# Second attention of a six-stage network: sums over the values in blocks of four steps instead of two, with eight buffers of probabilities instead of six

## The reference, cut to what matters

```
q, k = rope(x @ w_q.T), rope(x @ w_k.T);  v = x @ w_v.T
p = softmax(q @ k.T / sqrt(8))            # 512 x 512 for each head
out = x + concat_heads(p @ v) @ w_o.T
```

## Time and profile before

| | |
|---|---|
| time, median of 3 runs | 1658.82 us (1653.32 to 1661.22) |
| profiled execution, its own time | 1665.16 us |
| its span | 1663.4 us |
| TensorE busy | 1481.2 us (89%) |
| VectorE busy | 1036.2 us (62%) |
| ScalarE busy | 913.6 us (55%) |
| second attention, first scores to last sums | 1217.33 to 1434.41 us |

### The profile page before, as it was taken

How to read it: one execution, slowest core, us unless ns; L and a number is a source line. 1 busy time by engine, 2 the same in 40 slices (tenths; PEclk the granted TensorE clock), 3 DMA queues, 4 the chain that set the end, 5 groups by cost and what they waited for, 6 DMA issues and landing times. The chain is left out here.

```text
span 1663.4 us, 23904 instructions
## 1 busy us (share of the span) xinstructions
PE 1481.2 (89%) x7768; PEld 679.3 (41%) x7768; DVE 1036.2 (62%) x2527; ACT 913.6 (55%) x1706; POOL 495.0 (30%) x429
## 2 busy tenths in 40 slices
PE   7899999899988989879999986899889999878995
PEld 3444444344433333324434442268422222336663
DVE  6677775111117999966667765934368988186653
ACT  6866666524668999641046673012218888533443
POOL 5202111000137998820012221035101221006881
PEclk9999999999999999999999998999879999799998
DMA  6112210300000000010021119111222220242333
GB/s 161 49 30 59 68 30 2 98 0 1 0 5 3 4 5 5 0 48 1 1 51 27 27 35 398 32 17 22 92 81 68 73 68 21 86 150 33 43 42 86
DMA packets 64079, 84.21 MB, mean 51 GB/s; under 512 B 12442, under 2 KB 54992, under 8 KB 61942
## 3 DMA queue, kind: packets, MB, share of 16 engines
q1 hardware_dynamic: 55814, 75.85, 14.9%
q0 software_dynamic: 8144, 6.85, 3.3%
HBM read 54.09 MB, written 24.08 MB: 47 GB/s over the span
## 5 line engine op out<-in xcount | busy, mean ns | idle before, releaser
L697 ACT ACTIVATE a_probs_sb<-a_t_ps 128x512 f32<-128x512 f32 x512 | 286.1, 597 | 102.3 <-PE a_t_ps L545 56.4
L798 DVE CUSTOM_DVE_ANT_0 a_biased<-a_s_ps,a_bias 128x512 f32<-128x512 f32 x256 | 165.2, 686 | 65.9 <-issue 65.7
L541 PE MATMUL a_t_ps<-a_stack 126*128 126x512 bf16 (+1 forms) x512 | 164.1, 394 | 18.0 <-ACT a_probs_sb L697 6.6
L805 DVE TENSOR_REDUCE a_least_sb<-a_s_ps 128x2 f32<-128x1024 f32 x128 | 153.1, 1221 | 24.6 <-PE a_s_ps L522 23.7
L1597 POOL TENSOR_TENSOR s_dbu<-s_du,s_bs 128x1024 f32<-128x1024 f32 x64 | 152.2, 2389 | 26.1 <-DVE s_h L1678 20.1
L522 PE MATMUL a_s_ps<-a_stack 96*128 96x512 bf16 (+1 forms) x512 | 148.8, 393 | 12.2 <-DMA a_stack<-a_stacks 8.2
L1678 DVE TENSOR_TENSOR_SCAN s_h<-s_ps,s_dbu 128x512 f32<-128x512 f32 x128 | 149.0, 1205 | 6.4 <-ACT s_ps L1460 6.4
L559 PE MATMUL a_o_ps<-a_probs_sb,a_vpad 128*16 128x512 f32 x1024 | 132.0, 611 | 0.1
L1209 PE MATMUL s_ps<-s_hc,ident 128*128 128x512 f32 x256 | 120.5, 592 | 1.2 <-DVE s_hc L1685 1.2
L2093 ACT ACTIVATE q_probs_sb<-q_s_ps,q_most_sb 128x512 f32<-128x512 f32 x128 | 86.5, 683 | 48.1 <-DVE q_most_sb L2171 47.2
L1460 ACT ACTIVATE s_ps<-s_delta,s_decay 128x511 f32<-128x511 f32 x128 | 85.8, 686 | 27.5 <-DVE s_h L1678 27.2
(11 more groups left out here) (525 smaller groups left out, 2780.8 us busy)
## 6 DMA issues: line engine op xcount, KB each, us to landing
x_wu<-in_x_wu SPq DMA_DIRECT2D x2, 4096.0 KB, 17.4
a_stacks<-a_p SPq DMA_DIRECT2D x16, 384.0 KB, 3.3
a_stack<-a_stacks SPq DMA_DIRECT2D x32, 192.0 KB, 3.9
a_stack<-a_stacks SPq DMA_DIRECT2D x64, 96.0 KB, 2.3
a_stacks<-a_p SPq DMA_DIRECT2D x16, 256.0 KB, 2.4
q_q<-q_q SPq DMA_DIRECT2D x32, 128.0 KB, 2.3
x_wd<-in_x_wd SPq DMA_DIRECT2D x2, 2048.0 KB, 33.3
c_w<-in_c_w SPq DMA_DIRECT2D x2, 2048.0 KB, 12.7
```

The costliest lines, as they stand in the source:

```text
L541: last = nc.tensor.matmul(out, operand(1, k, pair, e, TURNED_ROWS)[:, t * P:(t + 1) * P], operand(0, k, pair, e, TURNED_ROWS), start=True, ...
L697: nc.scalar.activation(probs[:, y % PROB_RING, e, :], bank("turned", y, e), ACT.Exp, scale=-1.0).then_inc(probs_ready, 1)
L798: nc.vector.tensor_tensor_reduce(out=biased[:, e, :], in0=s_ps[:, 2 * (x % 2) + e, :], in1=bias[:, h, at:at + N], scale=1.0, scalar=3.0e38 ...
L805: nc.vector.tensor_reduce(least[:, k % 2, both], s_ps[:, 2 * (x % 2):2 * (x % 2) + 2, :], axis=AX.X, op=ALU.min).then_inc(least_ready, 1)
```

## The change

The sums of four steps are made together, at x divisible by 4; the other even steps have none. The ring of probabilities grows from six to eight buffers, since the oldest of them are now read up to two steps later. Nothing is computed otherwise, and no instruction is added or removed.

```diff
-    LAG, SUM_LAG, PROB_RING, SUM_STEPS = (13, 4, 8, 4) if alibi else (14, 3, 6, 2)
+    LAG, SUM_LAG, PROB_RING, SUM_STEPS = (13, 4, 8, 4) if alibi else (14, 3, 8, 4)
...
                 i, s = divmod(x, BATCH_STEPS)
                 y = x - LAG
                 z = y - SUM_LAG
-                sums = 0 <= z < ATT_STEPS and z % 2 == 1
+                sums = 0 <= z < ATT_STEPS and z % SUM_STEPS == SUM_STEPS - 1
                 if sums:
-                    sum_values(z // 2)
+                    for pair in range(SUM_STEPS // 2):
+                        sum_values((z - SUM_STEPS + 1) // 2 + pair)
                 if s in between(i):
                     make_between(i, s)
                 if not sums and x < ATT_STEPS:
```

## The result

The changed kernel is slower: 1678.16 us in the median (1676.02 to 1679.14) against 1656.88 us before, a ratio of 1.0122 with a 95% interval of 1.0102 to 1.0143. Measured again, with more runs of both, it was 1676.14 against 1658.44, 1.0103 (1.0076 to 1.0129). So the change costs some 18 to 21 us; 9.5 were forecast. The first measurement lies 1.2 us above the upper end of the forecast's range, 1677, the second just inside. The forecast had the direction right and about half of the size.

What follows compares the result with a forecast made beforehand. PE and ACT were taken to wait on each other over a short ring. Batches +8.9 us, including the 6.4 saving less the tail's share, and tail +0.6 gave +9.5: 1658.8 to 1668.3 us, range 1655 to 1677.

Steps and rivals of the forecast that it cites:

- What bounds the stage, and the stalls: Second attention: PE and ACT wait on each other over a short ring of banks; product steps stall 0.80 us per four.
- The layout on PE: Four steps laid out from the sums' first matmul, checked against banks and reductions: +0.09 to +0.70 us each.
- The saving of 0.20 us for each merged block: Sums on PE: 0.11 from one block of 1.85 us against two of 0.98, plus one 0.09 entry; 6.4 us over 32 blocks.
- the signs that were named: Profile of the changed kernel: among others, ACT's tile waits above 26.1 us over three batches, PE's busy time in batches lower.
- The tail: Stretch without scores after the last batch, 26.9 us before: some 32 at the low clock (+4.9) or 23.3 at full (-3.6).
- I take the middle, +0.6: Tail: the trace could not tell low clock (+4.9) from full clock (-3.6), so +0.6 us was entered.
- The difference carries over unscaled: Whole kernel: +9.5 us on the profiled execution, 6.3 above the runs' median, was added unchanged to 1658.8 us.
- The first and last batch: Second attention: first batch +0.5 us, its sums beginning at step 20 instead of 18; last batch +3.0 us.
- The first, stalls absorbed: Batches: PE's own stream is the bound, stall under 0.20 us per four steps; 1652 to 1660 us, chance 0.36.
- The second, the tail at the full clock: Tail keeps the full clock (-3.6) and batches save all 6.4: -10, 1649 us; chance 0.04.
- The third, the clock falling in the batches: Batches: granted clock falls as PE's busy share drops; some 5 us per 10 at the lower level, 1675 to 1690; chance 0.08.
- The fourth, the buffers: Ring of probabilities: more buffers help by themselves; ACT does not wait for sums, so put at nothing; no chance given.

Runs made afterwards that it cites:

- shortened exponentials: Changed kernel, and kernel before, with exponentials over 256 of 512 queries: four product steps 6.43 us instead of 6.81 (changed), two 3.11 against 3.12 (before).
- the repeated profile: The kernel before, unchanged, profiled again: stage 246.3 us against 252.1 in its first profile, tail 16.0 against 21.6, timed ratio 0.9999.
- fillers: Changed kernel with one 128x256 matmul without use at x = 129, 133, 137, 141 of the tail: tail 17.5 us, ratio to before 1.0082.
- fours at the ends: Kernel before with eight buffers and blocks of four steps in the first batch, from x = 100 on and in the tail: stage 255.5 us, ratio 1.0078.
- fours in the middle: Kernel before with eight buffers and blocks of four steps only from x = 36 to 96: stage 255.2 us, ratio 1.0035.
- shorter reductions: Changed kernel with reductions over 256 of 512 keys of each score tile, run once: four steps without between pieces 5.19 us instead of 5.44.

## Why the prediction was right or wrong

**What bounds the stage, and the stalls: right.** The layout on PE gave 6.83, 6.08, 5.46, 6.50, 6.07 and 7.0 us for four steps with products, with the extremes and the sums turned, without pieces, with heads and output, with values, and with the next batch's parts copied. Measured in the changed kernel at the full clock: 6.81, 5.98 to 6.04, 5.44, 6.47, 6.06 and 6.96. A middle batch grew by 2.4 us, 2.7 were forecast, and the shortened exponentials and reductions show the two causes. The saving of 0.20 us for each merged block is in these numbers and was not measured by itself. Two of the signs that were named did not come: ACT's waits for tiles did not grow (25.2 us against 26.1), and PE's busy time in a batch rose instead of falling.

**The tail: the step that failed.** "I take the middle, +0.6" rested on a tail of before of 26.9 us, from a profile in which the clock had fallen. In three of five profiles it stayed up, and that stretch is 21.4 us in the repeated one. The timed runs say that this is the usual case: outside this stage ten profiled executions on the chips where the kernel before ran at 1658 us took 1408.6 to 1413.1 us, 1412 in the middle, and the median of 1658.4 less 1412 leaves 246.4 for the stage (an estimate). The changed tail was put at 23.3 with the full clock and some 32 with the lower, without a working; it is 25.6 and 26.6, with single blocks at the lower clock and others not. Against 21.4 the first is +4.2, not +0.6. With fillers it is 24.7, of which its first block at the lower clock is 1.3, so 23.3 is about right for the full clock. "The difference carries over unscaled" failed with it: the profiled execution of before was 6.3 us over its median, with a stage 5.8 us longer than in the repeated profile.

Against the profile that it was read from the sum came out at +9.5 and the profiled execution at +10.8 us. That is partly luck: the batches were put 3.1 us too low, and the tail, which against the fallen one of 26.9 got 1.3 us shorter, 1.9 too high.

**The first and last batch: mis-sized, by the clock.** 0.5 and 3.0 us were forecast; by the parts of the table 2.7 and 3.6 were measured (53.1 - 50.3 and 48.8 - 45.2), and from block to block, as the layout counts, 1.9 and 4.4. In both a block of sums ran at the lower clock:

```profile
1245.26 3.61 PE L559 MATMUL a_o_ps<-a_probs_sb,a_vpad 128*16 128x512 f32 x16
1248.81 0.61 PE L541 MATMUL a_t_ps<-a_stack 51*128 51x512 bf16 x2
...
1390.37 3.42 PE L559 MATMUL a_o_ps<-a_probs_sb,a_vpad 128*16 128x512 f32 x16
1393.73 0.39 PE L541 MATMUL a_t_ps<-a_stack 51*128 51x512 bf16 x2
```

The second takes 3.36 us to the next start instead of 1.85. Without these 1.5 us the last batch is +2.9, so its layout was right at the full clock; fours at the ends, with no block at the lower clock there, agree. The first takes 3.55; the kernel before, whose blocks at x = 18 and 20 were partly low in the repeated profile, lost only 0.7 us there. The clock in the first batch was not in the layout at all.

**The rivals.** The first, stalls absorbed, was wrong: in four steps with products PE stalled 5.22 - 4.44 = 0.78 us (start of the second product against when PE was free for it in the layout), where this rival needed less than 0.20. The second, the tail at the full clock, did not come about in either profile of the changed kernel. The third, the clock falling in the batches, had 0.08 and a price of 5 us for each 10 at the lower level; it happened in part, at two blocks in each profile of the changed kernel, and cost 1.7 + 1.5 = 3.2 us. The fourth, the buffers, was worth nothing, as said. Counted in one line, from the repeated profile of before to the first of the changed: 2.7 + 2.4 + 2.4 + 3.7 + 4.2 = 15.4 us from the first scores to the last sums, plus 1.3 around them (0.4 ahead, 0.9 behind), which the forecast put at nothing: 16.7 us of stage.

Still open is when the clock falls. The same program lost it in the tail in one profile and kept it in another, and the middle blocks lost it near x = 52, and in part at x = 84, in two profiles (fours in the middle, and shorter reductions, 52.9 and 52.4 us for its middle batches), at places where six other profiles with blocks of four steps there did not.

## What to carry to other kernels

Merging blocks of one kind saves their entry and exit, but look at what the block was covering: between two uses of a short ring its length is free cover for the reader, and the step that loses it waits. Lay out one period by hand with the ring's rule and the starts of the timeline; here that gave each period at the full clock within 0.1 us. Before the sum is made against a stage of one profile, check that stage's granted clock, above all where the engine has gaps.

## What the runs showed of the hardware

The column-packed matmuls of the sums cost 0.98 us to the next start for 8 and 1.85 for 16, so 0.11 us of each block does not grow with its length (8 more cost 0.87). The granted clock of a tail that was the same in both executions was 1.00 in one and 0.68 in the other, 5.6 us apart, and in the latter it stayed at half for some 17 us while PE was listed as 95% busy. The gaps of PE ahead of that stretch, 0.71 and 0.57 us, were the same in both. One matmul without use at x = 17, behind a wait of 2.1 us, did not prevent the lower clock at the block of x = 20: the clock fell while it ran, and it is listed with 1.69 us. A float32 matmul has two records in these traces and a bfloat16 one a single record; the two passes named ahead of the prediction are these records, and no run here shows how often the data cross the array.
